# A mixer's output stage: the newest normalised rows are turned ahead of the projection of the unit in front

## What is computed

```python
y = y * z                                   # gated mixer output
y = y @ out_w.T + out_b
attn = jnp.clip(y + residual, -10.0, 10.0)
x = x + ga * attn
h = _layernorm(x, axis=-1) * (1 + cb) + sb  # the newest normalised rows
x_flat = jnp.einsum('bsd,de->bse', h, W_proj) + b_proj
router_logits = x_flat @ W_gate             # 8 experts, each row goes to one
```

## Time and profile before

| | us |
|---|---|
| median of 3 runs | 294.24 (293.84 to 294.24) |
| the profiled execution's own time | 293.55 |
| its span | 291.7 |
| TensorE busy / its share | 254.6 / 87% |
| VectorE busy / its share | 217.8 / 75% |
| GpSimd busy / its share | 181.5 / 62% |
| ScalarE busy / its share | 153.2 / 53% |
| first out-projection of the stage to the last logits copied | 89.9 to 127.1 |

### The profile page before, as it was taken

The page is one execution under the profiler, slowest core; times in us unless marked ns, Lnnn a source line. Parts: engine busy times, 40 slices in busy tenths (PEclk is TensorE's granted clock), DMA queues, the critical chain, the costliest instruction groups (busy, mean ns, idle before and its releaser), DMA issues.

```text
span 291.7 us, 6443 instructions
## 1 busy us (share of the span) xinstructions
PE 254.6 (87%) x1755; PEld 165.4 (57%) x1756; DVE 217.8 (75%) x870; ACT 153.2 (53%) x390; POOL 181.5 (62%) x224
## 2 busy tenths in 40 slices
PE   0998888798989999897889999999999999999630
PEld 0555555588867677553435565566565656655430
DVE  7799996998945999897355877777777777768530
ACT  3669666492513587579116554555444554446420
POOL 5679996100660666410475788888888888886560
PEclk9999999999999999999999999999999999999985
DMA  6940189930839799980132222222322222230000
GB/s 153 231 145 2 39 240 281 271 89 12 227 77 352 209 334 293 288 241 2 55 108 54 70 90 83 68 73 70 85 86 76 72 68 70 82 87 30 20 7 0
DMA packets 47314, 35.31 MB, mean 121 GB/s; under 512 B 4582, under 2 KB 42589, under 8 KB 47162
## 3 DMA queue, kind: packets, MB, share of 16 engines
q1 hardware_dynamic: 42312, 24.71, 30.7%
q0 software_dynamic: 3744, 9.77, 11.7%
q10 hardware_dynamic: 1234, 0.53, 0.7%
HBM read 24.34 MB, written 11.08 MB: 121 GB/s over the span
## 4 chain that ended last, share of the span: by engine, by line
PE 63%; POOL 9%; ACT 7%; DMA 5%; issue 5%; DVE 4%; SPq 4%; POOLq 0%; ACTq 0%; DVEq 0%
PE PS L1546 14%; PE PS L1529 12%; PE PS L1537 7%; PE PS L1531 4%; POOL rs L541 4%; PE PS L1283 4%; PE PS L1519 3%; PE PS L1455 3%; PE PS L1427 2%; ACT SBk L792 2%; DMA BIG<-k_pad 2%; DMA X<-in_L_attn_x_dram 2%; PE PS L1423 2%; PE PS L1363 2%; PE PS L1548 2%
## 5 line engine op out<-in xcount | busy, mean ns | idle before, releaser
L829 ACT ACTIVATE V<-PS,gb1T 128x128 f32<-128x128 f32 x156 | 58.7, 457 | 59.0 <-PE PS L1537 57.6
L615 POOL DMA_INDIRECT SBk<-rows,idgi x39 | 41.8, 1073 | 24.0 <-DVE idsi L1189 16.4
L1546 PE MATMUL PS<-BIG,V 128*128 x312 | 47.1, 291 | 1.6 <-DVE Wst L1241 0.9
L624 POOL DMA_INDIRECT out_dram<-Wst,idsi x39 | 39.8, 1021 | 11.1 <-DVE Wst L1252 7.4
L1546 PEld LDWEIGHTS PS<-BIG,V 128*128 128x128 f32 x312 | 43.3, 195 | 4.0 <-issue 2.2
L1235 DVE TENSOR_SCALAR V<-PS,mv,rs 128x512 f32<-128x512 f32 x39 | 31.4, 806 | 17.6 <-POOL rs L634 17.1
L1529 PE MATMUL PS<-BIG,V 128*128 x78 | 40.7, 603 | 3.0 <-issue 2.1
L634 POOL TENSOR_TENSOR rs<-ve,half 128x2 f32<-128x2 f32 x42 | 30.6, 729 | 12.5 <-DVE ve L1256 11.0
L1225 DVE BATCH_NORM_STATS2 st<-PS 128x6 f32<-128x512 f32 x39 | 27.1, 695 | 7.6 <-PE PS L1531 7.2
L1537 PE MATMUL PS<-ident,V 128*128 128x128 f32 x156 | 25.5, 286 | 1.7 <-ACT V L829 1.7
L586 POOL TENSOR_TENSOR Hh<-Hh,outb 128x1024 f32<-128x1024 f32 x4 | 9.5, 2420 | 22.8 <-ACT SBk L739 22.8
(11 more groups left out here) (256 smaller groups left out, 521.5 us busy)
## 6 DMA issues: line engine op xcount, KB each, us to landing
BIG<-k_pad SPq DMA_DIRECT2D x32, 256.0 KB, 5.6
BIG<-in_L_ffn_W_dram SPq DMA_DIRECT2D x1, 2048.0 KB, 9.4
rows<-GL SPq DMA_DIRECT2D x4, 512.0 KB, 4.5
rows<-Hh SPq DMA_DIRECT2D x8, 256.0 KB, 4.4
out_dram<-Hh SPq DMA_DIRECT2D x8, 256.0 KB, 4.6
rows<-U SPq DMA_DIRECT2D x4, 512.0 KB, 4.0
X<-in_L_attn_x_dram SPq DMA_DIRECT2D x3, 512.0 KB, 6.4
Wst<-la_rows SPq DMA_DIRECT2D x1, 1024.0 KB, 5.2
```

The costliest lines, as they stand in the source:

```text
L615: pool.indirect_dma_start(out=XG[:, u, :], out_offset=None, in_=rows, in_offset=bass.IndirectOffsetOnAxis(ap=idgi[:, t:t + 1], axis=0), bo ...
L624: pool.indirect_dma_start(out=out_rows, out_offset=bass.IndirectOffsetOnAxis(ap=idsi[:, t:t + 1], axis=0), in_=FO[:, t % RING, :], in_offs ...
L829: a.activation(AT[:, u, k, :], PS[:, 3, P * k:P * k + P], ACT.Gelu, bias=gb1T[:, 1, bass.ds(e, 1), k], scale=gb1T[:, 0, bass.ds(e, 1), k]) ...
L1546: m.matmul(dst, AT[:, u, k, :], W2s[:, bass.ds(e, 1), k, :].rearrange("p a d -> p (a d)"), start=(k == 0), stop=False)
```

## The change

In the loops of the output stage two calls change places, on both engines, for units 0 to 6. TensorE turns unit n before it projects unit n - 1, and ScalarE copies the turned rows of unit n before it copies the projection of unit n - 1. Unit 7 keeps its order. No instruction is added, removed or resized, and no semaphore changes.

```diff
@@ block.scalar: for q in range(2 * B + LAG + 1), n = q - LAG
                 early = 2 * B - DVE_NORMS <= n < 2 * B
                 if early:
                     turned2(n)
+                if 0 <= n < 2 * B and not early:
+                    turned2(n)
                 if n >= 1:
                     projected(n - 1)
-                if 0 <= n < 2 * B and not early:
-                    turned2(n)
@@ block.tensor: the same loop
                 if early:
                     rows_turn2(n)
                     fill(4, MOD[:, 0].rearrange("p b d -> p (b d)"), 1)
+                if 0 <= n < 2 * B and not early:
+                    rows_turn2(n)
                 if n >= 1 and not early:
                     project(n - 1)
-                if 0 <= n < 2 * B and not early:
-                    rows_turn2(n)
```

## The result

The changed kernel takes 302.38 us (median of 4, 302.1 to 305.62) against 294.24 us before (median of 4, 293.84 to 295.45): ratio 1.029, 95% interval 1.0233 to 1.0347. It is slower, as forecast, but by 8.1 us where 6.2 to 6.4 were forecast, and outside the range. Another 4 executions, taken beside the later experiments, have a median of 304.16 against 294.38: ratio 1.037 (1.033 to 1.0409). Medians here are of all executions of a kernel, while the ratios leave out those more than 1.5% above its fastest, which are two of unit 6 swapped and one, the profiled one, of normalising ahead.

A forecast was written before the change was run, and what follows sets the result against it. TensorE was taken as the bound, without a gap in the stage. Waits returning each round add 6.44 us: 299.99 from the profiled execution, 300.68 from the median; forecast 300.4 us, range 298.7 to 301.6.

The forecast's parts named there:

- the circle: Output stage: TensorE and ScalarE wait for each other every round, 4.89 instead of 4.08 us; assignment 6.44 us later; chance 0.91.
- A first wait: Round q = 3: unit 1's turn waits 0.82 us for ScalarE's normalised rows, delaying the next round by 0.97 us.
- round q = 7: Round without gated rows to turn: the turn comes 2.47 us in and the round ends at 4.42 us.
- 2.4 us gap before unit 6's turn: Round q = 8, end of the stage: TensorE has nothing to do until unit 6's turn, idling some 2.4 us.
- paid once: Rival for the rounds: ScalarE gets ahead again after the first, so only one wait is paid, 294.8 us; chance 0.03.
- faster: Rival: the three gaps at the stage's end, 1.06 us, go and no new one comes, 293.2 us; chance 0.03.
- the step of 0.59 us: TensorE, each round: from a turn that had to wait to the projection's first matmul, taken as 0.59 us.
- a queue that is passed: Rival: the projection's first weight load is done during the wait, 0.44 instead of 0.59 us, 299.1 us; no separate chance given.
- the rest moves as a whole: From the first assignment to the end: everything comes 6.44 us later, with the same length as before.
- the term for the clock: Rival: gaps bring TensorE to 1.2 GHz, a round 3.6 us more; 304 us for one, 315 for four; chance 0.03.
- The prediction's own sign of being wrong: Turns starting at once, rounds of 4.1 us, an assignment before 122, or a clock under 1.00 between 98 and 130.
- the base: Whole kernel's time before, to which 6.44 us is added: profiled execution 293.55 us or median 294.24; forecast 300.4, between both sums.

The follow-up runs named there:

- unit 6 swapped: Kernel before with both engines' calls swapped for unit 6 alone, units 0 to 5 in the old order: 297.28 us against 294.05, ratio 1.008.
- normalising ahead: Changed kernel's TensorE order, with ScalarE normalising unit n + 1 ahead of copying the projection of unit n - 1: 298.63 us against 294.05 before, ratio 1.0104.
- the kernel with its gap filled: Changed kernel plus two groups of spare matmuls on TensorE in front of unit 6's turn: 301.12 us against 294.3 before, ratio 1.0206.
- TensorE's order alone: Kernel before with only TensorE's calls swapped, ScalarE's order as before: 306.68 us against 294.3, ratio 1.0392.
- both gaps filled: Changed kernel plus two groups of spare matmuls before unit 6's turn and two before the last tile's turn: 300.76 us against 294.05 before, ratio 1.0203.
- unit 6 swapped and filled: Kernel before with only unit 6 swapped on both engines, plus two groups of spare matmuls before its turn: 296.81 us against 294.38, ratio 1.0089.
- ScalarE's order alone: Kernel before with only ScalarE's calls swapped, TensorE's order as before: 297.32 us against 294.3, ratio 1.0097.

## Why the prediction was wrong, by its own steps

**Right: the circle.** A first wait that makes the first round 0.97 us longer (measured 102.85 - 97.80 = 5.05 us against 4.08), rounds of 4.89 us (4.89), 2.47 us to the turn in round q = 7 (120.00 - 117.53), a 2.4 us gap before unit 6's turn (2.30), 6.44 us in all (6.43 with the clock held up). The idle time before the turns is 0.75 us and then 0.59, 0.59, 0.59 and 0.55, at the low end of the 0.65 to 0.8 expected and under it, as the profile counts it from the modelled end of the matmuls before. The rival "paid once" is what a kernel does that normalises ahead, and "faster" is excluded. Both halves were tested alone, and the two places apart.

**Right: the step of 0.59 us** from a waiting turn to the projection: it is 101.49 - 100.90 = 0.59 in the first round and within 0.01 of that in the others. The rival of a queue that is passed, from which 299.1 would have followed, shows no effect at this place. But its 0.44 was no bound for this pair: that is the step from a turn to the next gated turn. The same pair without a wait takes 105.45 - 104.92 = 0.53 us (normalising ahead), so of the 0.15 us only 0.06 came with the wait.

**Right: the rest moves as a whole.** From the first assignment to the last tile's down-product the kernel with its gap filled takes 151.81 us (127.41 to 279.22) against 152.01 before. The places where the filled kernels are longer than before from the assignment on are those where the clock fell.

**Wrong: the term for the clock.** It was priced as slow rounds of 3.6 us each, given 0.03, and had nothing in the sum. The step that failed is the one that dismissed it: "from 134 to 139 us TensorE is busy 2.75 of 5.00 us, and the granted clock is 1.00 all the while". The row is right, but its longest single idle stretch is 1.74 us:

```profile
137.45 1.04 PE L1511 MATMUL PS<-SBk 128*128 128x117 bf16 x16 [1.74 <-ACT SBk L802]
```

My own schedule had a gap of 122.52 to 124.99, 2.47 us, before unit 6's turn, and between the first and the last matmul of before no idle stretch is that long. (TensorE idles 6.84 us ahead of its first matmul, and the windows show 1.00 there too; that is before any change of the clock is on record.) A busy share over 5 us said nothing about one long gap. Nor was one passage without a fall a safe sample: behind the same 1.74 us at the same place, the clock did fall in four of the later profiles, 2.0 to 2.2 us after its end. What the runs showed in place of the dismissed term is a fall to 0.50 in or behind the gap before unit 6's turn in both profiles of the changed kernel, which cost 1.69 and 0.41 us of the stage, and a second one at the last tile in the first of them, 1.28 us. The prediction's own sign of being wrong, a clock under 1.00 between 98 and 130 us, showed itself.

The fall needed a price of its own: the gap's followers at twice their length, 1.12 and 0.63 and 2.18 instead of 0.66 and 0.40 and 1.19 us, at most 1.7 us (0.46 + 0.23 + 0.99 = 1.68). With it the forecast from the median, 300.68, becomes 301.1 (the second profile's 0.41) to 302.4 (the first's 1.69), and the range reaches past 303.

**Also wrong: the base.** I took the value between the profiled execution's sum (299.99) and the median's (300.68). The runs of before spread over 3 us with their mean clock (all but one at 0.980 to 0.983 up to 293.5 us, all but one at 0.975 to 0.978 from 294.6 us on), so the profiled one, at 0.983, was a good execution and not a typical one. The median was the base to use. Two small things beside it: the lower bound of the range, 299.1 less 0.3, is 298.8 and not 298.7, and the 0.2% that a measurement was said to tell from no change was too fine, as the interval of the result is 0.57% to either side.

The rule on small idle gaps that swing the clock (the Trainium skill, TensorE: Matmul & The Clock Gate, A second HAM failure mode: psum-queue depth-cycling) would have had the clock fall in the rounds. In none of the five profiles with rounds of 4.89 us did it fall before the last of these rounds had ended. Where it fell in the stage, it fell in or behind the one long gap. But the filled kernel's fall at 130 us, below, is nearer to that rule than to a single long gap.

What stays open is the part of the excess that no single profile shows: the second series of the changed kernel has 304.16, 3.3 more than the sum of waits from the median (294.38 + 6.44). Its profiled execution, 301.86, was its fastest, with a fall at 157 us as well as the one in the stage, so the slower ones aren't explained by a trace; their mean clocks (0.959 to 0.964 against 0.973) say only that the clock was down for longer. An estimate from them: 0.960 of a span of 302.2 us means 2 x 0.040 x 302.2 = 24 us at half speed, and 0.973 of 299.3 us means 16. At most half of the 8 us between them, 4 us, is lost time, which is enough for the 2.75 us between those two executions (304.61 and 301.86).

## What to carry to other kernels

Where two engines hand work to each other in fixed orders, write down the circle (who waits behind whom, around and back) and sum it before moving a step ahead of its neighbour: a step that was the other engine's cover becomes its wait, and the wait comes back each round. Changing the order on both sides alike doesn't help if the producer still stands behind the consumer's last copy; producing one unit further ahead takes the wait out of the rounds (though here the kernel stayed slower than before, for its end). And when a schedule on paper shows a new idle stretch on TensorE that is longer than any it had between its matmuls, price the matmuls behind it at half speed as well.

## What the runs showed of the hardware that was not expected

The clock fell to 0.50 in or behind idle stretches of 2.30 us (in both profiles of the changed kernel), 2.35 and 2.78 us, and behind one of 1.44 us (normalising ahead). At two shorter stretches, which nearly every profile has, it was now up and now down. Behind the 1.74 us of the earlier trace rows it stayed at 1.00 in before, but fell 2.0 to 2.2 us after its end, with another 0.71 us of idle time between, in TensorE's order alone (151.2), both gaps filled (147.1), unit 6 swapped and filled (141.1) and normalising ahead (144.5). At the 1.73 us before the last tile it stayed up in before and in the second profile of the changed kernel, and fell in the first (284.1) and in the kernel with the gap filled (283.7). When it fell, it was during the gap (123.7), or up to 1.6 us behind its end (126.1 and 121.8), and 2.2 us behind the 1.74 us of the earlier trace rows. It also fell without any gap over 0.9 us: in the kernel with both fills at 130.0, after five microseconds in which TensorE was busy 4.04 us, and with ScalarE's order alone at 151.3, behind 3.85 us of 5.00:

```profile
146.00:151.00 5.00, 3.85 (x10) 1.19 (x9) 1.45 (x5) 0.69 (x3) 3.52 (x5) 1.00 0.46 146
151.00:152.00 1.00, 0.76 (x1) 0.50 (x2) 1.00 (x4) 0.10 (x1) 0.70 (x1) 0.64 0.00 0
```

Whether a given idle stretch brings the clock down thus differs from execution to execution, and one profile is a sample. The executions' mean clocks show it well: with unit 6 alone swapped, the three at 0.983 took 295.05 to 295.59 us, the four at 0.971 to 0.973 took 296.8 to 297.74, and the three at 0.960 to 0.964 took 298.68 to 300.54. (0.983 is also the mean of the profiled execution of before, where the clock fell only at 281.6, behind the last matmul.)
